# The second layer of a small vision transformer in a new order: keys shuffled on VectorE, the second chunk's projections beside the first one's scores, the softmax weights' eviction on ScalarE, the end in halves

## What is computed

```python
x = layernorm(h)
qr, qi, kr, ki, v = (heads(x @ W.T) for W in (Wqr, Wqi, Wkr, Wki, Wv))
sr = (qr·kr + qi·ki) * scale
si = (qi·kr - qr·ki) * scale
probs = softmax(sqrt(sr*sr + si*si))
h = h + probs @ v
x = layernorm(h)
route_prob = softmax((x @ enc_w + enc_b) @ sw_w + sw_b)       # 8 experts, best one taken
h = h + route_prob.max() * (gelu(x @ w1[e] + b1[e]) @ w2[e] + b2[e])
```

## Time and profile before

| | us |
|---|---|
| median of 3 runs (476.99 to 482.29) | 478.06 |
| profiled execution | 476.72 |
| its span, first to last instruction | 475.0 |
| busy: TensorE, VectorE, ScalarE, GpSimd | 429.8, 276.5, 201.1, 95.8 |
| layer two starts (first sum of experts' rows) | 275.36 |
| scores of chunk 0, 1, 2, 3 start | 297.84, 333.90, 377.18, 419.32 |
| mean granted TensorE clock | 0.977 |

### The profile page before, as it was taken

One profiled execution on the slowest core, in us unless ns is written; L12 is line 12 of the kernel. 1 busy time (PEld: TensorE's weight loads), 2 busy tenths in 40 slices (PEclk: granted clock), 3 DMA queues, 4 the chain that ended last, 5 costly groups with the idle time before them and its releaser, 6 DMA issues.

```text
span 475.0 us, 11871 instructions
## 1 busy us (share of the span) xinstructions
PE 429.8 (90%) x4000; PEld 374.8 (79%) x4001; DVE 276.5 (58%) x987; ACT 201.1 (42%) x433; POOL 95.8 (20%) x137
## 2 busy tenths in 40 slices
PE   6999999985899999999999579778998999999885
PEld 6899999875899999999999466656677668667745
DVE  4478888876245454454554565686677373654711
ACT  1343433521144453453553302762882486179130
POOL 3114655555211311212212211011010000100100
PEclk9999999997799999999999979999999999999999
DMA  7999704203111211212212162000001000000000
GB/s 225 327 401 397 255 33 131 63 28 120 45 41 38 64 39 42 62 39 49 61 39 48 46 198 68 3 2 1 1 1 28 1 3 14 13 3 1 2 26 27
DMA packets 30063, 35.45 MB, mean 75 GB/s; under 512 B 9295, under 2 KB 25359, under 8 KB 30027
## 3 DMA queue, kind: packets, MB, share of 16 engines
q1 hardware_dynamic: 25095, 28.52, 19.1%
q0 software_dynamic: 3072, 4.95, 3.2%
q10 hardware_dynamic: 1860, 1.49, 1.0%
HBM read 27.19 MB, written 9.14 MB: 76 GB/s over the span
## 4 chain that ended last, share of the span: by engine, by line
PE 72%; DVE 10%; ACT 8%; issue 4%; DMA 3%; POOL 1%; SPq 0%; POOLq 0%; DVEq 0%; ACTq 0%
PE ps L869 13%; PE ps L837 9%; PE ps L684 7%; PE ps L896 6%; PE ps L848 5%; PE ps L1017 4%; PE ps L1005 3%; PE ps L908 2%; PE ps L937 2%; PE ps L922 2%; PE ps L972 2%; PE ps L728 2%; PE ps L671 2%; ACT squares L1247 2%; PE ps L738 1%
## 5 line engine op out<-in xcount | busy, mean ns | idle before, releaser
L869 PE MATMUL ps<-w,hidT 128*128 x384 | 65.1, 326 | 0.0
L869 PEld LDWEIGHTS ps<-w,hidT 128*128 128x128 f32 x384 | 62.0, 190 | 0.0
L638 POOL DMA_INDIRECT ys_dram<-ys,y_place_now x32 | 31.1, 972 | 116.9 <-DVE ys L1682 112.0
L837 PE MATMUL ps<-xsT,low_now 128*128 128x128 f32 x384 | 49.8, 279 | 0.2 <-ACT xsT L1179 0.2
L1203 ACT ACTIVATE hidT<-ps,b_act_now 128x128 f32<-128x128 f32 x96 | 28.2, 364 | 51.3 <-issue 49.0
L837 PEld LDWEIGHTS ps<-xsT,low_now 128*128 128x128 f32 x384 | 46.1, 191 | 2.4 <-ACT xsT L1179 0.5
L594 POOL TENSOR_TENSOR rstd<-meanvar,eps 128x2 f32<-128x2 f32 (+1 forms) x24 | 5.2, 216 | 202.7 <-DVE meanvar L1807 101.0
L671 PE MATMUL ps<-ident 128*128 128x128 f32 x196 | 31.7, 327 | 12.7 <-DMA y_first<-ys_dram 8.2
L671 PEld LDWEIGHTS ps<-ident 128*128 128x128 f32 x196 | 29.8, 238 | 13.9 <-issue 13.3
L684 PE MATMUL ps<-w_tok,patches 128*128 128x192 f32 x192 | 36.0, 343 | 4.7 <-DMA patches<-in_patches 4.7
L1667 DVE TENSOR_SCALAR hidT<-ps,b_dve_now 128x128 f32<-128x128 f32 x96 | 27.7, 344 | 21.3 <-PE ps L848 21.3
(11 more groups left out here) (219 smaller groups left out, 805.0 us busy)
## 6 DMA issues: line engine op xcount, KB each, us to landing
patches<-in_patches SPq DMA_DIRECT2D x7, 768.0 KB, 8.0
w<-in_W SPq DMA_DIRECT2D x8, 576.0 KB, 11.6
xs<-xs_dram SPq DMA_DIRECT2D x36, 96.0 KB
w_low<-in_W_low SPq DMA_DIRECT2D x8, 384.0 KB, 10.9
w_high<-in_W_high SPq DMA_DIRECT2D x8, 192.0 KB, 11.4
y_first<-ys_dram SPq DMA_DIRECT2D x4, 384.0 KB, 3.6
y_second<-ys_dram SPq DMA_DIRECT2D x4, 384.0 KB, 4.3
out<-out_tok SPq DMA_DIRECT2D x8, 150.0 KB
```

Of the source, the lines that this page charges most:

```text
L638: nc.gpsimd.indirect_dma_start(out=ys_dram[:, :], out_offset=bass.IndirectOffsetOnAxis(ap=y_place_now[v][:, 0:1], axis=0), in_=ys[v][:, :] ...
L837: mm = pe.matmul(ps[:, 4 + 2 * v + m // 3, P * (m % 3):P * (m % 3) + P], low_now[v][:, P * m:P * m + P], xsT[v][:, 0, :], start=(starts an ...
L869: mm = pe.matmul(ps[:, 2 * v + 1, 0:D], hidT[v][:, m, :], w2[:, bass.ds(experts[v], 1), D * m:D * m + D].rearrange("p e n -> p (e n)"), st ...
```

## The change

The edits, all in layer two:

1. The mapped keys' matmuls and evictions go. VectorE evicts each key group twice: once scaled by `part_sign` (+1 or -1 by partition, the row sums of `to_kk`), once by `stream_shuffle`, which swaps the 16 real and 16 imaginary partitions in each block of 32. ScalarE scales the queries by the same sign. One semaphore step stands for both copies.
2. In chunk 0, chunk 1's transposes stand behind scores 0 (banks 6, 7), its second group of queries and keys behind scores 1, its third behind scores 2, its first behind scores 3. The two `keep_awake(5, 8)` go.
3. Chunk 2's sum of experts' rows moves on VectorE from behind chunk 0's shifts to between chunk 0's key groups; its statistics follow the value evictions, its norm the first sum of squares. Chunk 3's norm moves ahead of the output of chunk 0.
4. ScalarE evicts the whole of a tile's transposed weights, 768 columns over two banks, in one instruction; VectorE none. In chunk 0 exponentials and these evictions alternate, and chunk 1's query evictions stand between roots and exponentials.
5. Values are released after each of their two banks.
6. The root's table is loaded by a dummy before layer two, the Gelu's in the last chunk by a dummy behind the switch exponential.
7. In the last chunk variance, inverse root and norm go two tiles at a time, transposes tile by tile; the last output is stored in two halves, each by two transfers.

```diff
+SWAPPED = [*range(DH, 2 * DH), *range(DH)]
...
+        def order_of(c, j):
+            return (3, 1, 2)[j] if c == 1 else j + 1
...
+                def store(c, tiles):
                     for half in range(2):
                         sp.dma_start(
-                            out[CT * c:CT * c + CT, :].rearrange("(i two t) d -> two t i d", two=2, t=T)[half],
-                            out_tok[c % 2][HALF * half:HALF * half + T, :, :]).then_inc(out_done[c % 2], 16)
+                            out[CT * c:CT * c + CT, :].rearrange("(i two t) d -> two t i d", two=2, t=T)[half][:, tiles, :],
+                            out_tok[c % 2][HALF * half:HALF * half + T, tiles, :]).then_inc(out_done[c % 2], 16)
...
                 def scores(c, i):
                     if i == 0:
-                        pe.wait_ge(kk_act_done, 2 * c + 2)
-                        pe.wait_ge(kk_dve_done, c + 1)
+                        pe.wait_ge(q_done, 3 * c + 3)
+                        pe.wait_ge(k_done, 3 * c + 3)
+                        if c:
+                            pe.wait_ge(pT_done, TILES * c)
...
                             elif i == 1:
-                                pe.wait_ge(q_done, 3 * (c + 1) + 1)
-                                pe.wait_ge(k_done, 3 * (c + 1) + 1)
+                                pe.wait_ge(q_done, 3 * (c + 1) + (1 if c else 3))
+                                pe.wait_ge(k_done, 3 * (c + 1) + (1 if c else 2))
...
                     scores(c, 0)
                     if later_ffn:
                         encode(c - 1)
+                    else:
+                        turn(2, 0, 6, 2)
                     scores(c, 1)
...
-                    if not later_ffn:
-                        keep_awake(5, 8)
+                    else:
+                        queries_keys(1, [1])
                     scores(c, 2)
                     if later_ffn:
                         turned_choice(c - 1)
+                    else:
+                        queries_keys(1, [2])
                     scores(c, 3)
-                    if not later_ffn:
-                        keep_awake(5, 8)
...
-                        queries_keys(c + 1, EARLY[c])
+                        queries_keys(c + 1, range(1))
...
-                turn(3, 1, FFN[c][0], CHUNKS)
+                for i in range(TILES):
+                    pe.wait_ge(x_done[3], CHUNKS + i)
+                    for g in range(2):
+                        mm = pe.transpose(ps[0:FG, FFN[c][0] + g, P * i:P * i + P],
+                                          x_tok[1][:, i, FG * g:FG * g + FG], ident[:, :])
...
# ScalarE
-                    nc.scalar.copy(probsT[i % 2][:, 0:3, :], ps[:, 2 * (i % 2), 0:3 * P]).then_inc(pT_act_done, 1)
+                    nc.scalar.copy(probsT[i % 2][:, :, :].rearrange("p (b r) k -> p b (r k)", b=2),
+                                   ps[:, 2 * (i % 2):2 * (i % 2) + 2, 0:3 * P]).then_inc(pT_done, 1)
...
+                nc.scalar.activation(table_warm[:, :], ident[:, 0:1], ACT.Sqrt)
                 turned(2, 0, 0, 1)
...
                     square(c, 0)
...
+                    else:
+                        turned(2, 0, 6, 2)
                     square(c, 1)
...
                     root(c, 2)
-                    if more:
+                    if c and more:
                         turned(2, 0, 0, c + 2)
+                    if c == 0:
+                        queries(1, [1, 2])
                     root(c, 3)
...
+                    weights(c, 0)
+                    if c:
+                        switch_exp(c - 1)
+                    else:
+                        queries(1, [0])
+                    weights(c, 1)
+                    if c == 0:
+                        turned_weights(c, 0)
+                    weights(c, 2)
+                    if c == 0:
+                        turned_weights(c, 1)
+                    weights(c, 3)
+                    for i in range(0 if c else 2, TILES):
                         turned_weights(c, i)
...
                 switch_exp(c)
+                act.wait_ge(s_exp_done, CHUNKS)
+                nc.scalar.activation(table_warm[:, :], ident[:, 0:1], ACT.Gelu)
...
# VectorE
                 def keys(c, groups):
...
-                        nc.vector.tensor_copy(kk[:, j, :, 0, :], packed(ps[:, 3 + 2 * j, 0:CT])).then_inc(k_done, 1)
+                        nc.vector.tensor_scalar(kk[:, j, :, 0, :], packed(ps[:, 3 + 2 * j, 0:CT]), part_sign[:, 0:1], None, ALU.mult)
+                        nc.vector.stream_shuffle(kk[:, j, :, 1, :], packed(ps[:, 3 + 2 * j, 0:CT]), SWAPPED).then_inc(k_done, 1)
...
+                def last_normed(half):
+                    dve.wait_ge(xT_in_psum[3], 2 * CHUNKS - 2)
+                    dve.wait_ge(rstd_done[3], CHUNKS + half)
+                    for i in range(2 * half, 2 * half + 2):
+                        nc.vector.tensor_scalar(x_tok[1][:, i, :], h_tile(CHUNKS - 1, i), meanvar[1][:, i, 0:1],
+                                                rstd[1][:, i:i + 1], ALU.subtract, ALU.mult).then_inc(x_done[3], 1)
...
                 add_experts(1)
-                keys(0, range(1))
+                keys(0, [0])
                 normed(1)
-                keys(0, range(1, HG))
+                keys(0, [1])
+                add_choice(2, 0)
+                keys(0, [2])
+                add_choice(2, 1)
                 high_values(0)
-                mapped_keys(0)
+                experts_stats(2)
...
                     add_squares(c, 0)
                     if c:
                         route(c - 1)
+                    else:
+                        normed(2)
...
-                    if c + 2 < CHUNKS:
-                        add_experts(c + 2)
-                    if more:
-                        keys(c + 1, EARLY[c])
+                    if c == 0:
+                        keys(1, [2, 0])
+                    if c == 1:
+                        add_experts(3)
+                    if c and more:
+                        keys(c + 1, range(1))
+                    if c == 1:
+                        normed(3)
...
-                    turned_weights(c, 0)
                     for i in range(TILES):
-                        if i + 1 < TILES:
-                            turned_weights(c, i + 1)
                         context(c, i)
-                    attended_norm(c)
+                        if c == 0 and i == 0:
+                            keys(1, [1])
+                        if not more and i == 1:
+                            last_variance(0)
```

More of the change, by code:

```diff
@@ L647, in _ @@
                     inverse_deviation(2, c)
-                for c in range(CHUNKS):
+                for c in range(CHUNKS - 1):
                     if c + 2 < CHUNKS:
@@ L651, in _ @@
                     inverse_deviation(3, c)
+                for half in range(2):
+                    of = slice(2 * half, 2 * half + 2)
+                    rooted(meanvar[1][:, of, 1], rstd[1][:, of], CHUNKS + half, var_done[3], eps_added[3], rstd_done[3])
             @block.tensor
@@ L1053, in _ @@
                         pe.wait_ge(squares_done, TILES * c + TILES)
+                    if later_ffn and more:
                         turn(2, 0, 0, c + 2)
@@ L1227, in low_values @@
                     for bank in range(2):
+                        act.wait_ge(v_in_psum, 2 * c + bank + 1)
                         last = nc.scalar.copy(
@@ L1323, in _ @@
                         gelu(c - 1)
-                    if more:
-                        queries(c + 1, EARLY[c])
-                    for i in range(TILES):
-                        weights(c, i)
-                        if c and i == 0:
-                            switch_exp(c - 1)
-                    for i in range(TILES):
+                    if c and more:
+                        queries(c + 1, range(1))
+                    weights(c, 0)
[11 more added lines that the diff above has]
+                    for i in range(0 if c else 2, TILES):
                         turned_weights(c, i)
@@ L1742, in high_values @@
                     for bank in range(2):
+                        dve.wait_ge(v_in_psum, 2 * c + bank + 1)
                         last = nc.vector.tensor_copy(
@@ L1851, in output @@
                             h_tile(c, i), ALU.mult, ALU.add)
-                    if half:
+                    if half or c == CHUNKS - 1:
                         last.then_inc(out_ready, 1)
```

137 lines of the change are left out of this document (62 added, 75 removed).

## The result

The changed kernel takes 460.82 us, the median of 4 runs (459.65 to 465.33); the kernel before, beside it, took 478.08 (476.99 to 482.29). The ratio is 0.964, with a 95% interval of 0.959 to 0.969. The forecast was 459.5 in a range of 456 to 464. The profiled execution took 459.67 with a span of 457.9, against 476.72 and 475.0: 17.1 us less span, where the prediction's sum had 17.85.

The account below looks back on a forecast made before the run. TensorE, busy nine tenths of the span, was taken as the bound; terms 8.9+3.55+2.4+1.5+0.5+1.0 = 17.85 us off the profiled 476.72 gave 458.9, or 460.2 like the median; forecast 459.5, range 456 to 464.

Parts of the forecast that it names:

- the terms of the first scores: Chunk 0's keys: 292.2+1.05+1.41+0.5+0.55 = 295.75, shuffle at 0.5, first scores released 2.1 us earlier.
- Chunk 0, step by step: Replay of chunk 0 in the new order until chunk 1's scores start at 325.0 instead of 333.90: 8.9 us gained.
- One lead: Chunk 0: four exponentials at 315.27 run one after the other before TensorE goes on; hole of 1.26 us.
- The root's table: Chunk 0's scores: loading the table early removes a 1.28 us load between two scores.
- Chunk 1: Gain 3.55: mapped keys 2.12, first-product wait 0.98 and last-product wait 0.43 by ScalarE's eviction; moving the norm gives nothing.
- Theory B: Experiments' counter-theory: clock and VectorE's order decide, so terms overlap or new waits cost more than one execution shows; no size.
- Chunks 2 and 3, the end: Gains: chunk 2 2.4, last chunk's norm and transposes 1.5, early Gelu table 0.5, split last store 1.0.
- Shuffles near 1.0: Rival: an unseen mask load makes each shuffle near 1.0 us, four on the path; 462, chance 9%.
- VectorE holding more of chunk 0: Rival: chunk 0's slacks of 0.2 to 0.4 all fail, 3 us more, store gives 0; 463.5, chance 6%.
- The change not doing what it says: Rival: an unseen wait holds chunk 0's end, only mapped keys' 2x2.12 gained; 472.5 or 473.8, chance 3.5%.
- The clock in chunk 0: Rival: the clock falls after chunk 0's waits of 1.9 and 2.5, 1.5 us each; 462.5, chance 8%.
- The slower rival: Clock falls in chunk 0 and stays low through chunks 0 and 1; 500, slower than before, chance 2%.

Follow-up runs that it names:

- evict_alone: The kernel before with only ScalarE evicting each tile's whole turned weights, VectorE none; 477.88 us, ratio 0.996.
- evict_undone: The changed kernel with the weights' eviction shared between ScalarE and VectorE again; 469.96 us in one run, beside 489.89 for before.
- tables_end_undone: The changed kernel without early root and Gelu table loads, last norm and transposes for four tiles at once, last output stored whole; 465.24 us, ratio 0.970.
- shuffle_alone: The kernel before with only the mapped keys replaced by shuffles and sign scaling; 475.2 us, ratio 0.988.
- order_undone: The changed kernel with chunk 0's old order, keep-awake matmuls back, chunk 3's norm still moved; 466.27 us, ratio 0.973.
- shuffle_twice: The changed kernel with each of the 12 shuffles done twice, first into a spare buffer; 470.82 us in one run.
- late_norm: The changed kernel with eight extra VectorE multiplications ahead of chunk 0's normed tokens, lengthening TensorE's wait; 470.41 us in one run.
- after_again: The changed kernel run once more, unedited, in a later series; 465.32 us, ratio 0.964 to the kernel before.
- order_undone_2: The same kernel as order_undone, run again: the changed kernel with chunk 0's old order; 472.36 us, ratio 0.981.

## Why the prediction was right

**Time and sum.** The seven stretches gained 17.39 where the terms gave 17.85. The missing 0.5 lies in chunk 0, and layer two began 0.29 later in the profiled execution. That execution took 459.67 where the sum gave 458.9 for its like, the median 460.82 where it gave 460.2; so the number did not come out by errors that cancel. Two sums are slightly off as written and move nothing: the terms of the first scores give 295.71, not 295.75, and those of chunk 1 3.53, not 3.55.

**Chunk 0, step by step** (0.29 taken off each time of after). First scores 295.87, predicted 295.75: the shuffle at half a microsecond and the order on VectorE are right. Scores 2 began at 301.72 (301.5) and scores 3 at 305.43 (305.1): a projection group took 2.89 to the next scores, not 2.7, twice. The first weights' turn began at 311.98 (311.6). Tile 1's began at 313.14 and waited for its exponential, not for VectorE's keys as the step had it. Values ended at 321.75 (321.45), VectorE's four contexts with a key group took 6.43 (6.33), variance to norm 1.78 (1.8), the last wait 2.72 (2.5), and the transposes 1.07 instead of 0.96 to chunk 1's scores. Together 8.37 against 8.9. The term was mis-sized mainly in two rows, the projection group and the transposes; the mechanism holds. One lead was misread: TensorE did not wait for all four exponentials, it turned the first weights at 316.03, while they ran until 317.76. It was the first product that stood behind them. And each run of keep-awake records, 16 of them, is 8 matmuls.

**Shares of the 8.37.** Undone one by one, the order is worth 3.6 and the eviction 0.9. What is left, 3.8, goes with the shuffle, the mapped keys of chunks 0 and 1 among it; that remainder is a difference and was not measured by itself.

**The root's table: wrong reason, no harm.** "With the table loaded early there is no 1.28 here" gave the early load a part that it does not have. The projection groups behind scores 1 and 2 pace this stage, and the load would have stood in ScalarE's wait. The replay itself said that the square no longer sets the pace; it should have struck the table from the list.

**Chunk 1: right size, shared cause.** The prediction gave 0.98 of the wait to the eviction and "nothing" to the norm's move. evict_alone measured the first (1.45 for chunk 1, with the 0.43), but evict_undone only 0.50: the 1.23 is gone in both, and by VectorE's list it is the norm's move that removes it in the second. This is where Theory B is right. The sum did not notice, since both edits were in.

**Chunks 2 and 3, the end.** 2.40, 1.52, 0.51 and 1.05 against 2.4, 1.5, 0.5 and 1.0. tables_end_undone gives the three of the end as 1.28, 0.52 and 0.89, and evict_undone gives chunk 3 another 0.54. Of the last norm's 1.5 the step gave 0.3 to the eviction; 1.52 less 1.28 is 0.24, but undoing the eviction alone costs 0.54, so these two overlap as well. That the Gelu table is worth 0.5 and not its 1.28 holds, since the last hidden matmul then sets the outputs. ScalarE's timeline shows the load under the switch network, and the dummy 0.02 after it:

```profile
441.26 1.28 ACT L1357 ACT_TABLE_LOAD   x1
442.56 0.20 ACT L1357 ACTIVATE table_warm<-ident 128x1 f32<-128x1 f32 x1
```

The Trainium skill (ScalarE: Activation LUTs, What ACT_TABLE_LOAD costs) has a drain of 1.38 us beside the load; these rows disagree, since the next instruction follows at once, and the measurement decides. Nor is there one ahead of a load: in chunk 0 of the changed kernel the last root ends at 310.20 and the exponential's load starts at 310.22.

**Rivals.** Shuffles near 1.0: refuted by the 0.52 step. VectorE holding more of chunk 0: refuted, its four contexts took 0.1 more than replayed, and the 0.4 by which they began late came from TensorE. The change not doing what it says: refuted by the stretches. The clock in chunk 0 was underpriced, at 1.5 for a fall. It did not fall from 296.16 to 447.64 in the profiled execution (the end stretch has 0.94, as before), but it fell in chunk 0 or at the start of chunk 1 in the profiles of shuffle_alone, evict_alone, order_undone, tables_end_undone, shuffle_twice, late_norm and after_again. Where the same order was also seen at 1.00, it cost 4.7 (tables_end_undone), 3.1 (after_again) and 38.0 - 33.38 = 4.6 (order_undone). Three of the seven profiles, shuffle_alone, evict_alone and order_undone, keep the old order with its keep-awake matmuls, so it is no price of this change alone; the ratio holds from series to series (0.9641 and 0.9642). The slower rival had the fall, but not what follows it: in none of these profiles did the clock stay down into chunk 2.

## What to carry to other kernels

Replay the path of the stage that has slack, instruction by instruction, with durations from the trace, and price by start to start rather than by a record's length. A load or an eviction is worth its length only where its engine has no idle time in the **new** order; ask this again after the replay. When two edits each remove the same wait, the sum counts it once, and undoing one of them says little about the other.

## What the chip showed that was not expected

**The clock is not a function of the wait.** The same wait of 2.72 us before the same transposes was followed by a granted clock of 1.00 in one execution and by 0.50 (1.2 GHz) for some 9 us in another; waits of 1.44 and 0.29 were followed by 12 us at 0.50 in a third. Before the longest, 6.01, it fell while TensorE was still idle, in the one execution seen. Identity matmuls in that wait kept it at 1.00, in one execution as well. With the old order it fell behind shorter ones too: 1.26 and 1.07 in order_undone, 1.26 and 0.91 in shuffle_alone, 1.08 in evict_alone, while order_undone_2 stayed at 1.00 with the same 1.26 and 1.08. What decides in the short cases stays open: these runs don't tell it.

**Cost of a fall.** In chunks 0 and 1 it was 1.4 (shuffle_twice) to 4.7 us, and less where waits for other engines follow, because slower matmuls fill them. In evict_alone's network stretch, 16 us at 0.50 behind a wait of 1.54, it was 18.43 - 11.51 = 6.9.

**Weights' eviction over two banks.** One ScalarE copy of 768 columns took 0.80, which is what the linear estimate between 384 and 1200 columns gave. A query eviction with a scale by partition took 0.60 where the plain one took 0.50 before; these are rows of the changed kernel's groups (busy, mean ns, idle before).

```profile
L1270 ACT COPY probsT<-ps 128x768 f32<-128x768 f32 x16 | 12.5, 800 | 13.2 <-PE ps L964 13.2
...
L1229 ACT ACTIVATE q<-ps,part_sign 128x400 f32<-128x400 f32 x12 | 7.1, 598 | 14.7 <-PE ps L909 14.7
```
